# Expert stage of a gated cross-attention kernel: blocks of w1 stand in the array while the rows stream

## The reference, cut to what matters

```
x_rep = x[token_ids]                       # 4096 rows: each of the 2048 rows twice
for e in range(E):                         # E = 8
    h1 = x_rep @ w1[e].T                   # w1[e]: 704 x 128
    a, g = jnp.split(h1, 2, axis=-1)       # 352 and 352
    he = jax.nn.silu(a) * g @ w2[e].T      # w2[e]: 128 x 352
    out = out + jnp.where((expert_ids == e)[:, None], he, 0)
out = out * scores.reshape(-1, 1)
combined = out.reshape(N, TOP_K, h).sum(axis=1)
```

## Time and profile before

| | us |
|---|---|
| three runs | 469.72, 472.52, 472.85 |
| their median | 472.52 |
| span of the profiled execution | 471.6 |
| expert stage in it: first load of a tile issued to last scatter landed | 348.5 to 456.3 |
| PE busy, whole span | 339.0 (72%) |
| DVE busy | 260.9 (55%) |
| ACT busy | 140.6 (30%) |
| POOL busy | 96.5 (20%) |

### The profile page before, as it was taken

How to read it: one execution, slowest core, us unless ns; L and a number is a source line. 1 busy time by engine, 2 the same in 40 slices (tenths; PEclk the granted TensorE clock), 3 DMA queues, 4 the chain that set the end, 5 groups by cost and what they waited for, 6 DMA issues and landing times.

```text
span 471.6 us, 5266 instructions
## 1 busy us (share of the span) xinstructions
PE 339.0 (72%) x1327; PEld 198.6 (42%) x1329; DVE 260.9 (55%) x753; ACT 140.6 (30%) x310; POOL 96.5 (20%) x156
## 2 busy tenths in 40 slices
PE   1157645545899899999789996862019999999930
PEld 0157521132333434444343553532006777777720
DVE  4748986997336513759862786475702333333314
ACT  1021025452141222333322243311013545455510
POOL 8400000017100000000033002414321334334430
PEclk9999955565555555999955897985557999999975
DMA  8991013900000000000000000101011111111127
GB/s 248 328 330 28 2 8 70 303 0 1 2 0 0 0 1 0 0 1 0 0 18 30 0 0 12 37 11 35 24 47 30 54 44 55 51 52 51 39 58 217
DMA packets 30192, 25.79 MB, mean 55 GB/s; under 512 B 8362, under 2 KB 26273, under 8 KB 30171
## 3 DMA queue, kind: packets, MB, share of 16 engines
q1 hardware_dynamic: 26011, 12.56, 10.2%
q0 software_dynamic: 4160, 12.99, 8.1%
HBM read 11.35 MB, written 14.49 MB: 55 GB/s over the span
## 4 chain that ended last, share of the span: by engine, by line
PE 56%; DVE 26%; issue 7%; DMA 4%; POOL 4%; ACT 2%; SPq 1%; POOLq 0%; DVEq 0%; ACTq 0%
PE wide L630 12%; PE bank L663 7%; PE wide L756 6%; PE bank L771 5%; PE wide L757 5%; PE bank L651 3%; PE wide L629 3%; PE bank L764 3%; DVE st L814 2%; DVE amh L965 2%; DVE h L843 2%; DVE space L961 2%; DMA space<-expert_out 2%; DVE rv L830 1%; POOL expert_rows L339 1%
## 5 line engine op out<-in xcount | busy, mean ns | idle before, releaser
L339 POOL DMA_INDIRECT expert_rows<-pay,slot x32 | 30.8, 964 | 194.8 <-DVE slot L1082 186.3
L630 PE MATMUL wide<-kblk,h2T 32*128 32x308 f32 x128 | 69.5, 633 | 0.0
L663 PE MATMUL bank<-pTC,vblk 128*128 128x512 f32 (+1 forms) x80 | 53.3, 758 | 10.6 <-ACT pTC L427 10.6
L991 DVE TENSOR_REDUCE mC<-wide 128x8 f32<-128x616 f32 x32 | 25.5, 798 | 60.3 <-PE wide L630 60.0
L348 POOL DMA_INDIRECT expert_out<-space x39 | 38.3, 982 | 70.7 <-DVE space L1137 70.7
L1131 DVE TENSOR_TENSOR space<-space,wide 128x352 f32<-128x352 f32 x39 | 20.3, 521 | 58.6 <-PE wide L757 55.9
L419 ACT ACTIVATE space<-space 128x616 f32<-128x616 f32 x32 | 22.8, 716 | 91.3 <-DVE space L994 91.3
L756 PE MATMUL wide<-w_s,space 128*128 x78 | 32.5, 499 | 3.7 <-issue 2.9
L515 PE MATMUL bank<-ident,h 128*128 128x128 f32 x48 | 13.3, 432 | 29.8 <-DVE h L843 29.0
L771 PE MATMUL bank<-w_s,space 128*128 (+1 forms) x234 | 32.8, 276 | 1.0 <-DVE space L1137 1.0
L651 PEld LDWEIGHTS bank<-ident,space 128*128 128x128 f32 (+1 forms) x160 | 23.6, 166 | 22.9 <-issue 18.6
(11 more groups left out here) (209 smaller groups left out, 512.2 us busy)
## 6 DMA issues: line engine op xcount, KB each, us to landing
expert_rows<-blank POOLq DMA_DIRECT2D x2, 2970.0 KB, 19.2
w_s<-in_w1T SPq DMA_DIRECT2D x1, 2816.0 KB, 10.0
expert_rows<-blank POOLq DMA_DIRECT2D x1, 2574.0 KB, 29.8
space<-expert_rows SPq DMA_DIRECT2D x39, 66.0 KB, 1.8
space<-expert_out SPq DMA_DIRECT2D x8, 256.0 KB, 3.1
xs<-in_x SPq DMA_DIRECT2D x4, 256.0 KB, 5.1
w_s<-in_w2T SPq DMA_DIRECT2D x2, 512.0 KB, 11.9
out<-xs SPq DMA_DIRECT2D x4, 256.0 KB, 3.3
```

Source lines behind the costliest of these rows:

```text
L339: pool.indirect_dma_start(tbl, bass.IndirectOffsetOnAxis(ap=slot[:, k, t:t + 1], axis=0), pay[:, b % 2, k, j, :], None).then_inc(rows_sent ...
L630: ins = pe.matmul(o, qT[r, b, j * P:(j + 1) * P], kblk[r, :, b * KS:(b + 1) * KS], start=False, stop=True)
L663: pe.matmul(bank[1][:], vblk[0:w, c, b, :], pTC[0:w, q % 2, :], start=(c == 0), stop=(c == NCH - 1)).then_inc(pv_done, 1)
L991: link(dve.tensor_reduce(m.rearrange("p (g l) -> p g l", g=2), s, AX.X, ALU.max))
```

## The change

In the expert stage the two operands of the up product change places. Blocks of 128 columns of w1 stand in the array, and the transposed tile `mhT` streams: three blocks for each half, six matmuls of 128 columns for two of 352. The product then has the hidden columns on the partitions and tokens along the free dimension, which is the form that the down product needs, so `e_TH` and ACT's two copies are gone. Since 352 is not a multiple of 128, the third block starts at column 224 and repeats 32 columns; the corresponding 32 partitions of w2's third piece are zero (a memset on POOL), and w2's last 96 rows are loaded to partitions 32 to 127. ACT's silu and DVE's multiplication work on 384 columns where they worked on 352.

w1 no longer lies in SBUF. SP brings the tile's w1 (128 x 704 floats, 352 KB) from HBM into a ring of WRING = 4 buffers `w1r`, one load for each tile. A buffer comes free when the up product of the tile four before is done (`e_w1`). SP's loop now issues w1 of tile 8k+j+4 and then the rows of tile 8k+j+8. PE reads the places in w2 for eight tiles at the head of its loop from the new table `w2at`. PE's order is T(i+2), up(i+1), down(i). The transposed tile has two PSUM banks for one, and so has the down product.

```diff
-        w1_s = sb("w1_s", [P, E * 2 * F]); w2_s = sb("w2_s", [P, E * NF * D])
+
+
+        LAP = NF * P - F
+        F0 = [0, P, F - P]
+        WRING = 4
+        w1r = sb("w1r", [P, WRING, 2 * F])
+        w2_s = sb("w2_s", [P, E * NF * D])
...
+        w2at = sb("w2at", [1, NTILE], I32)
...
-        msil, mhid, mhidT = reuse(2, F), reuse(2, F), reuse(2, NF, P)
+        msil, mhidT = reuse(2, NF, P), reuse(2, NF, P)
...
-            sp.dma_start(w1_s[:].rearrange("p (e f) -> p e f", e=E), w1T.rearrange("e d f -> d e f")).then_inc(ld_exp, 16)
             w2v = w2_s[:].rearrange("p (e c d) -> p e c d", e=E, c=NF)
             for c, (f0, n) in enumerate(FC):
-                sp.dma_start(w2v[0:n, :, c, :], w2T[:, f0:f0 + n, :].rearrange("e f d -> f e d")).then_inc(ld_exp, 16)
+                sp.dma_start(w2v[P - n:P, :, c, :], w2T[:, f0:f0 + n, :].rearrange("e f d -> f e d")).then_inc(ld_exp, 16)
+
+            def load_w1(i, q, buf=True):
+                e = sp.value_load(expi[0:1, bass.ds(i, 1)], min_val=0, max_val=E - 1)
+                if buf:
+                    sp.wait_ge(e_w1, i - WRING + 1)
+                sp.dma_start(w1r[:, q, :], w1T[bass.ds(e, 1), :, :].rearrange("e d f -> d (e f)")).then_inc(w1_load[q], 16)
+
+            def load_x(i, j, sent=None):
+                r = sp.value_load(rowi[0:1, bass.ds(i, 1)], min_val=0, max_val=NULL * P)
+                if sent is not None:
+                    sp.wait_ge(e_scat[j], 16 * sent)
+                sp.dma_start(mpay[:, j, :], tbl[bass.ds(r, P), :]).then_inc(e_load[j], 16)
 
             sp.wait_ge(turns_ready, 1)
+            load_w1(0, 0, False)
+            load_w1(1, 1, False)
             for k in range(2):
                 sp.wait_ge(rows_sent[k], 16 * NT)
-
-            def load(i, j):
-                r = sp.value_load(rowi[0:1, bass.ds(i, 1)], min_val=0, max_val=NULL * P)
-                sp.dma_start(mpay[:, j, :], tbl[bass.ds(r, P), :]).then_inc(e_load[j], 16)
-
-            for j in range(RING):
-                load(j, j)
-            with sp.Fori(1, NTILE // RING) as k:
+            for j in range(4):
+                load_x(j, j)
+            load_w1(2, 2, False)
+            load_w1(3, 3, False)
+            for j in range(4, RING):
+                load_x(j, j)
+            with sp.Fori(0, LOOPS - 1) as k:
                 for j in range(RING):
-                    sp.wait_ge(e_scat[j], 16 * k)
-                    load(RING * k + j, j)
-            for i in range(NTILE // RING * RING, NTILE):
-                sp.wait_ge(e_scat[i % RING], 16 * (i // RING))
-                load(i, i % RING)
+                    load_w1(RING * k + (j + WRING), j % WRING)
+                    load_x(RING * k + (j + RING), j, k + 1)
+            for i in range(RING * (LOOPS - 1) + WRING, NTILE):
+                load_w1(i, i % WRING)
+                if i + WRING < NTILE:
+                    load_x(i + WRING, (i + WRING) % RING, (i + WRING) // RING)
...
+            pool.memset(w2_s[0:LAP, :].rearrange("p (e c d) -> p e c d", e=E, c=NF)[:, :, NF - 1, :], 0.0).then_inc(lap_zero, 1)
...
-            def e_copy_hT(i, p):
+            def e_copy_hT(i, p, buf=True):
                 act.wait_ge(e_hT_psum, i + 1)
-                act.activation(mhT[:, p, :], bank[0][:, 0:P], ACT.Copy).then_inc(e_hT, 1)
-
-            def e_silu(i, p):
+                if buf:
+                    act.wait_ge(e_w1, i - 1)
+                act.activation(mhT[:, p, :], bank[3 * p][:, 0:P], ACT.Copy).then_inc(e_hT, 1)
+
+            def e_silu(i, p, buf=True):
                 act.wait_ge(e_gate, i + 1)
-                act.activation(msil[:, p, :], wide[:, 2 * p, 0:F], ACT.Silu).then_inc(e_sil, 1)
-
-            def e_copy_hidT(i, p):
-                act.wait_ge(e_hidT_psum, i + 1)
-                act.activation(mhidT[:, p, 0:2], bank[2 + p][:, 0:2 * P], ACT.Copy).then_inc(act_chain, 1)
-                act.activation(mhidT[0:FC[2][1], p, 2], bank[2 + p][0:FC[2][1], 2 * P:3 * P], ACT.Copy).then_inc(e_hidT, 1)
-
-            def slot_(i, j, has0=True, has1=True, buf=True):
-                if has1:
-                    act.wait_ge(e_hid, i)
-                    e_silu(i + 1, (j + 1) % 2)
-                if has0:
-                    act.wait_ge(e_w1, i + 1)
-                    e_copy_hT(i + 2, j % 2)
                 if buf:
-                    act.wait_ge(e_w2, i - 1)
-                e_copy_hidT(i, j % 2)
-
-            e_copy_hT(0, 0)
-            e_copy_hT(1, 1)
-            e_silu(0, 0)
-            act.wait_ge(e_w1, 1)
+                    act.wait_ge(e_hid, i - 1)
+                act.activation(msil[:, p], wide[:, 2 * p, 0:NF * P].rearrange("p (c t) -> p c t", c=NF),
+                               ACT.Silu).then_inc(e_sil, 1)
...
-            def e_T(i, j, k):
-
+            def e_T(i, p, j, k, buf=True):
                 pe.wait_ge(e_load[j], 16 * (k + 1))
-                if not (isinstance(i, int) and i == 0):
-                    pe.wait_ge(e_hT, i)
-                pe.transpose(bank[0][:, 0:P], mpay[:, j, 0:D], ident[:]).then_inc(e_hT_psum, 1)
-
-            def expert(i):
-                return pe.value_load(expi[0:1, bass.ds(i, 1)], min_val=0, max_val=E - 1)
-
-            def e_up(i, p, e):
+                if buf:
+                    pe.wait_ge(e_hT, i - 1)
+                pe.transpose(bank[3 * p][:, 0:P], mpay[:, j, 0:D], ident[:]).then_inc(e_hT_psum, 1)
+
+            def places(i, n):
+                _, vs = nc.values_load_multi_w_load_instructions(
+                    w2at[0:1, bass.ds(i, n)], engines=[mybir.EngineType.PE], min_val=0, max_val=(E - 1) * NF * D,
+                    skip_runtime_bounds_check_because="the vector engine takes the minimum with E - 1 before the product")
+                return vs
+
+            def e_up(i, p, q, k, buf=True):
+                pe.wait_ge(w1_load[q], 16 * (k + 1))
                 pe.wait_ge(e_hT, i + 1)
-                if not (isinstance(i, int) and i < 2):
+                if buf:
                     pe.wait_ge(e_hid, i - 1)
-                pe.matmul(wide[:, 2 * p, 0:F], mhT[:, p, :], w1_s[:, bass.ds(e * 2 * F, F)]).then_inc(e_gate, 1)
-                pe.matmul(wide[:, 2 * p + 1, 0:F], mhT[:, p, :], w1_s[:, bass.ds(e * 2 * F + F, F)]).then_inc(e_w1, 1)
-
-            def e_TH(i, p):
+                for g, done in ((0, e_gate), (1, e_w1)):
+                    for c in range(NF):
+                        ins = pe.matmul(wide[:, 2 * p + g, c * P:(c + 1) * P], w1r[:, q, g * F + F0[c]:g * F + F0[c] + P],
+                                        mhT[:, p, :])
+                    ins.then_inc(done, 1)
+
+            def e_down(i, p, w, buf=True):
                 pe.wait_ge(e_hid, i + 1)
-                if not (isinstance(i, int) and i < 2):
-                    pe.wait_ge(e_hidT, i - 1)
-                for c, (f0, n) in enumerate(FC):
-                    ins = pe.transpose(bank[2 + p][0:n, c * P:(c + 1) * P], mhid[:, p, f0:f0 + n], ident[:])
-                ins.then_inc(e_hidT_psum, 1)
-
-            def e_down(i, p, e):
-                pe.wait_ge(e_hidT, i + 1)
-                pe.wait_ge(e_y, i)
-                for c, (f0, n) in enumerate(FC):
-                    ins = pe.matmul(bank[1][:, p * P:(p + 1) * P], mhidT[0:n, p, c, :],
-                                    w2_s[0:n, bass.ds(e * NF * D + c * D, D)], start=(c == 0), stop=(c == NF - 1))
+                if buf:
+                    pe.wait_ge(e_y, i - 1)
+                for c in range(NF):
+                    ins = pe.matmul(bank[1 + p][:, 0:D], mhidT[:, p, c, :], w2_s[:, bass.ds(w + c * D, D)],
+                                    start=(c == 0), stop=(c == NF - 1))
                 ins.then_inc(e_w2, 1)
...
             with pe.Fori(0, LOOPS) as k:
+                w = places(RING * k + 1, RING)
                 for j in range(RING):
                     i = RING * k + 1 + j
-                    experts[j] = expert(i + 1)
-                    e_up(i + 1, j % 2, experts[j])
-                    e_T(i + 2, (j + 3) % RING, k + (j + 3) // RING)
-                    e_TH(i, (1 + j) % 2)
-                    e_down(i - 1, j % 2, experts[j - 2] if j >= 2 else expert(i - 1))
-            for i in range(RING * LOOPS + 1, NTILE + 1):
+                    e_T(i + 2, (j + 1) % 2, (j + 3) % RING, k + (j + 3) // RING)
+                    e_up(i + 1, j % 2, (j + 2) % WRING, 2 * k + (j + 2) // WRING)
+                    e_down(i, (j + 1) % 2, w[j])
...
+            dve.tensor_scalar(w2at[:], tE[:], float(E - 1), float(NF * D), ALU.min, ALU.mult).then_inc(turns_ready, 1)
...
             def e_mul(i, p, buf=True):
                 if buf:
-                    dve.wait_ge(e_hidT_psum, i - 1)
+                    dve.wait_ge(e_w2, i - 1)
                 dve.wait_ge(e_sil, i + 1)
                 dve.wait_ge(e_w1, i + 1)
-                dve.tensor_tensor(mhid[:, p, :], msil[:, p, :], wide[:, 2 * p + 1, 0:F], ALU.mult).then_inc(e_hid, 1)
-
```

(8 more changed lines are left out.)

61 lines of the change are left out of this document (36 added, 25 removed).

## The result

The changed kernel takes 483.36 us (median of 4 runs, 478.27 to 484.46), the kernel before 472.69 us beside it: a ratio of 1.025, 95% interval 1.016 to 1.035. It is slower, where 466.4 us and faster was forecast. Executions of one and the same kernel fall here into a faster group and one some per cent slower (x1_after: 472.89 to 478.12 and 482.01 to 485.99); ratios are taken from each set's faster runs, medians from all, and three of the changed kernel's first four, 483.23 to 484.46, lie where x1_after has its slower ones. So the loss is small, 0.1 to 3.5% by the two intervals, and more likely near 1%; the forecast's gain is absent in both.

The account below looks back on a forecast made before the run. The prediction saw the bound move from PE to SP, at 2.42 us a tile. Pace and faster drain gave 6.9 us less, contention took back 0.8: profile 471.6 to 465.5, median 466.4 us, range 461 to 474.

Parts of the forecast that it names:

- PE's own part: PE in the expert stage: twelve up-product passes in 1.34 us, weight loads hidden, 2.12 us a tile instead of 2.29.
- The head of PE's loop: PE's sequencer: one read at the head of eight tiles, about 0.3 to 0.5 us, covered by short waits.
- SP's pace: SP's queue in the expert stage: two load steps of 1.20 us and 0.02, so 2.42 us a tile, the new bound.
- The ring: Expert-stage loads: w1 of tile i+5 goes out behind the wait for tile i's scatter; at least 2.33 us a tile.
- the sum: Expert stage added up from first row load to last down product, ending at 446.6 against 453.5: 6.9 us less.
- the straight line between 66 and 2816 KB: Landing of a 352 KB w1 load, interpolated from 1.8 and 10.0 us: 2.65 us.
- the prediction's second figure: Landing of a w1 load by the skill's formula, about 2.0 us plus bytes at 436 GB/s: 2.8 us.
- the ring's landings come 0.5 us later in all: Contention allowance on expert-stage landings: 2.455 us a tile, 0.035 over SP's pace, 0.8 us over 23 tiles.
- the ring runs dry: Expert-stage DMA: scatter and w1 landings together over 2 us later, 2.83 us a tile or more, 478 us and up; chance 0.08.
- the gain is eaten: Expert stage: landings 0.9 to 2 us later or SP's steps 1.3 us, no change, 468 to 477 us; chance 0.27.
- P: Time of one turn, one tile, by the closed chain of expert-stage loads and scatters: at least 2.33 us, 2.455 with contention.
- The clock: PE in the expert stage: stays at 2.4 GHz; the rival, a fall from 0.3 us waits, 540 us, had chance 0.01.

Follow-up runs that it names:

- x1_after: The changed kernel run again, nothing altered, in eleven runs: 478.12 us, ratio 1.008 to the kernel before.
- x9: The changed kernel with w1 loaded for the first four tiles only, later tiles reusing those blocks: 464.09 us, ratio 0.982 to the kernel before.
- x13: The changed kernel with PE reading its places behind the first up product of a turn, not at its head: 478.34 us, ratio 1.017.
- x3: The changed kernel with rows loaded six tiles ahead instead of eight: 466.20 us, ratio 0.980 to the kernel before.
- x5: The changed kernel with eight buffers for w1 instead of four, loads issued eight tiles ahead: 470.91 us.
- x8: The changed kernel with rows loaded seven tiles ahead instead of eight: 467.64 us, ratio 0.990 to the kernel before.
- x6: The changed kernel with rows loaded six tiles ahead and SP reading eight values of each table at its loop's head: 468.03 us, ratio 0.975.
- x11: The changed kernel with w1 loads issued by ACT and PE reading its places behind a turn's first up product: 458.77 us, ratio 0.971.
- x12: x6 with PE reading its places behind the first up product of a turn: 457.65 us, ratio 0.971 to the kernel before.

## Why the prediction was wrong, step by step

- **PE's own part: right.** Twelve passes in 1.34 us, 0.112 apart, and 2.12 us a tile (x9's rows). The weight loads are hidden, also in this form: the rule of "TensorE: Matmul & The Clock Gate" of the Trainium skill, section "Part 3: Packing small matmuls", that the prediction weighed, by which they would be exposed, doesn't hold here. After a wait the up product takes 1.42 us instead of 1.34 from its start to the down product's (401.38 to 402.80 in the lap above): its first two passes stand 0.18 apart, about the 0.19 of a weight load.
- **The head of PE's loop: wrong, without effect here.** "About 0.3 to 0.5 us [...] the short waits below cover it". It is 1.0 to 1.2 us. In the changed kernel the waits do cover it (x13), and in the mended ones it costs 3.6 to 3.8 us.
- **SP's pace, 2.42 us: right as a number, wrong as the bound.** Where the ring is open, the tile is 2.36 to 2.42 (x3, x5, x8), and the stage 99.7 to 103.1 us against the 101.8 of the sum. In the changed kernel SP isn't the limit; it waits for scatters.
- **The ring: the failed step.** The chain was right, as x3_lead6 and x8_lead7 show by lengthening its distance and nothing else; its terms were mis-sized, so the prediction had SP as the bound where the ring was. Forecast 9.32 us for four tiles, measured 11.10. Scatter to row load: 2.2 and a wake-up of 0.17, measured 3.32. The w1 step: 1.36, measured 1.23. Its landing and PE's start: 2.95, measured 3.57. Up product, down product and DVE's part to the scatter: 2.64, measured 2.98. The excess is 1.78 us, 0.45 a tile.
- **What the excess is made of.** The landings themselves are 1.2 us: the scatter's 2.92 us for 2.2 (mean of the 10 in the trace), w1's 3.14 for 2.65. Up product to scatter is 0.34. About 0.36 are laps in which SP or PE came to a landed load late, PE mostly behind the stall at the head of its loop. The w1 step gives 0.13 back.
- **Why the landings were put too short.** For w1's the traffic is hardly the reason: a w1 load that goes out with no other under way takes 2.84 to 3.30 us (seven such at the starts of the changed kernel, x1, x5 and x9), so the straight line between 66 and 2816 KB was wrong there, and the stream adds little. So was the prediction's second figure for it, 2.8 us: section "Anatomy of one DMA" of "DMA: Bandwidth & Descriptors" of the Trainium skill gives that formula for DMAs issued from GpSimd, and SP issues these. "0.3 for PE to start" stood on no row and is 0.23. The allowance "the ring's landings come 0.5 us later in all" stood for what is 1.2 us. It was chosen without a row for it, though the DMA engines' share was to go from 0.17 to 0.60, with only 0.09 us a tile between the ring and SP's pace.
- **The rival was there and under-rated.** The slower one, "the ring runs dry", named the mechanism and got 0.08, "the gain is eaten" 0.27. Its point of decision, 2 us more of landings, was too late: 1.2 us, with 0.34 on the engines and the late laps, gave 2.71 to 2.80 us a tile. And the two rivals left a gap: by the prediction's own 0.25 us a tile, landings 0.9 to 2 us later make P 2.56 to 2.83, not "2.48 to 2.7", and the slower rival began at 2.83. Both measured paces lie between. "today's row loads all land within 1.7 to 1.9 us" was an argument from a kernel without the traffic.
- **The clock: right for the stage, not behind every wait.** From 365 to 445 us it stayed at 2.4 GHz, as forecast. Near the end it fell once. The scatter issued at 429.72 lets SP's row load go 3.65 us later, and the w1 behind it comes 2.31 us late for PE; some ten microseconds on it happens again, with 1.54. In the timelines of SP and PE of the changed kernel:

```profile
433.37 0.34 SPq L255 DMA_DIRECT2D space<-expert_rows  x1
434.46 0.34 SPq L249 DMA_DIRECT2D w1r<-in_w1T  x1
...
437.96 1.58 PE L775 MATMUL wide<-space,w1r 128*128 128x128 f32 x12 [2.31 <-DMA w1r<-in_w1T]
...
449.05 2.27 PE L775 MATMUL wide<-space,w1r 128*128 128x128 f32 x12 [1.54 <-DMA w1r<-in_w1T]
451.12 1.49 PE L784 MATMUL bank<-w_s,space 128*128 x6
```

The granted clock behind it, in the table by stages:

```profile
448.00:452.00 4.00, 2.95 (x17) 2.95 (x18) 0.54 (x1) 0.49 (x1) 0.77 (x1) 0.72 0.74 194
452.00:456.00 4.00, 4.00 (x32) 4.00 (x32) 1.27 (x4) 1.15 (x4) 1.24 (x2) 0.85 0.73 257
```

The clock's mean is 0.72 and 0.85: from 450 to 453 us it was at its lower level, 1.2 GHz, and the products of that tile took 2.27 and 1.49 us instead of 1.58 and 0.83. From this up product's start to the next transpose are 3.35 us for 2.09 behind the earlier wait, and the next tile takes 2.51 for 2.12, together 1.65 us; x1_after, whose stage is 2.6 us shorter, has no such fall. In x13_late the same came behind a wait of 2.87 us. The length of a wait alone doesn't decide it: behind the wait of 2.31 us above, and behind waits of 1.98 us in x1_after and 1.68 us in x13_late, the granted clock stayed at 1.00. "TensorE: Matmul & The Clock Gate" of the Trainium skill, section "HAM oscillation — how this bites in real kernels", describes how the array starts again at the lower clock behind waits for an operand's DMA. The traces agree for two of these five waits, at a mean of 0.72 and 0.68, and not for the other three.
- **The range** had "up to P of about 2.65" as its upper end. P was 2.71 to 2.80.

What stays open: why single scatters land late, as that of tile 25 in x1_after, 3.62 us behind its start, and that of tile 29 in the changed kernel, 3.84, where the kernel before has 2.2 in that stretch. The row loads behind such a one are late too, 3.8 to 4.1 us behind their scatters, but not by their own scatters: that of tile 27 in x1_after had landed after 2.78 us and its row load went 4.03 us behind it. In the changed kernel the row loads of tiles 33 to 36 go out 2.2 to 2.3 us apart, SP's own pace for its two steps, as it catches up. Nor was the gap between the changed kernel's two medians, 483.36 and 478.12, followed further, beyond the 1.65 us of the clock in the first profile.

## What to carry to other kernels

When a stream joins a queue that already waits for something, write down the closed chain through that wait and divide it by the number of tiles it spans; price its landings from rows of the same size and with the new traffic, and treat a margin of a few per cent as none. The cure here needed no less traffic: one tile of distance, or another engine's queue, took the old wait off the stream's path at no cost in traffic. Before undoing a change that lost, run its halves apart: here neither half lost, and only their order on one queue did.

## What the runs showed of the hardware

- Landings under load, by the medians of the table: with the stream running (DMA engines at a share of 0.60 to 0.76 from 380 to 400 us) a load of 66 KB took 2.3 to 3.1 us for 1.8 before, at a share of 0.17; a scatter 2.7 to 3.7 for 2.2; and a load of 352 KB 3.2 to 3.8, for 2.84 to 3.30 with no other w1 load under way. "DMA: Bandwidth & Descriptors" of the Trainium skill, section "Latency and other measured facts", has 0.2 us of HBM access on average and 2 us at high load. The rise measured here for row loads and scatters, 0.5 to 1.5 us, lies inside that span; no run here tells the memory's latency from waiting behind other transfers. In the prediction I had set this rule aside because the kernel before showed nothing of it.
- A stream of 198 GB/s into SBUF changed neither the time of float32 products (19.19 us of PE in 20 us against 19.21) nor the kernel's time (ratio 1.002).
- A register-addressed load costs SP 1.18 us a step with its value read singly, 0.5 to 0.6 us with eight read at once (x6), and the turn of the loop with its sixteen reads 3.5 us.
- Eight values read by PE at the head of its loop, 1.96 to 2.06 us on its sequencer, leave the array idle for 1.0 to 1.2 us in most turns; behind an up product of 1.34 us all but 0.3 us is hidden (x11, x12).
